# Eight tile buffers instead of five for the four-wide products, and another ring slot for the first prefetched unit

## What is computed

```python
x = layernorm(x + adj @ (scale[:, None] * (adj @ (x @ w0))) + bias)              # layer 0: two products with adj
x = layernorm(x + relu((inv_deg[:, None] * A1) @ x @ W.T + b))                     # layer 1: one
d = rsqrt(rowsum(adj)); z = leaky_relu((d[:, None] * (adj @ (d[:, None] * x))) @ W1 + b1)
S = exp(-sqrt(pairwise_squared_distances(z)) / 2), only the 4 nearest of each row kept
A2 = S + adj; d2 = rsqrt(rowsum(A2))
x = layernorm(x + (d2[:, None] * (A2 @ (d2[:, None] * x))) @ W2 + b2)             # layer 2: two, and a search
x = layernorm(x + relu(concat(x, adj @ x) @ W.T + b))                             # layer 3: one
```

## Time and profile before

| | us |
|---|---|
| median of three runs (lowest, highest) | 1589.72 (1587.08, 2805.07) |
| the profiled execution | 1597.85 |
| its span, first to last instruction | 1596.3 |
| TensorE busy (share of the span) | 1446.2 (91%) |
| VectorE busy | 836.0 (52%) |
| mean granted TensorE clock | 0.972 of full speed |

### The profile page before, as it was taken

The page is one execution under the profiler, slowest core; times in us unless marked ns, Lnnn a source line. Parts: engine busy times, 40 slices in busy tenths (PEclk is TensorE's granted clock), DMA queues, the critical chain, the costliest instruction groups (busy, mean ns, idle before and its releaser), DMA issues.

```text
span 1596.3 us, 20924 instructions
## 1 busy us (share of the span) xinstructions
PE 1446.2 (91%) x7300; PEld 748.6 (47%) x7300; DVE 836.0 (52%) x1278; ACT 465.3 (29%) x979; POOL 208.9 (13%) x267
## 2 busy tenths in 40 slices
PE   6888888887999999999999888999999499878997
PEld 4555555554444444444444433444444144433554
DVE  6667667664222133323222379999998046543122
ACT  4656565653000000000000056666665000000010
POOL 1111111110000000000000000000000447763000
PEclk9999999999999999999999999999999799989999
DMA  9999998888899888888777500013333889889773
GB/s 312 332 334 340 340 323 314 311 323 332 340 343 345 335 314 312 316 324 331 304 283 283 184 7 1 14 54 120 123 124 115 283 321 371 310 321 361 284 284 130
DMA packets 127677, 418.98 MB, mean 262 GB/s; under 512 B 10657, under 2 KB 44033, under 8 KB 104577
## 3 DMA queue, kind: packets, MB, share of 16 engines
q1 hardware_dynamic: 78272, 331.37, 55.9%
q0 software_dynamic: 19088, 71.83, 11.8%
q10 hardware_dynamic: 30256, 15.00, 3.2%
HBM read 353.14 MB, written 65.01 MB: 262 GB/s over the span
## 4 chain that ended last, share of the span: by engine, by line
PE 56%; DVE 16%; DMA 10%; issue 7%; POOL 5%; ACT 5%; DVEq 0%; ACTq 0%; POOLq 0%; SPq 0%
PE acc L1010 12%; PE acc L1011 12%; PE acc L1012 12%; POOL gath_all L434 5%; DVE hT L865 5%; DVE wz_sb L866 5%; DMA at_scratch<-region 4%; PE pt L1054 3%; DMA gath_all<-y_scratch,wz_sb 2%; DVE region L818 2%; PE pt L1116 2%; PE pt L1119 2%; PE pt L1118 2%; PE pt L1117 2%; PE pt L1012 2%
## 5 line engine op out<-in xcount | busy, mean ns | idle before, releaser
L1010 PE MATMUL acc<-region,yop 128*128 128x512 f16 x850 | 326.8, 385 | 63.7 <-DVE region L818 39.1
L1011 PE MATMUL acc<-region,yop 128*128 128x512 f16 x850 | 326.2, 384 | 0.0
L1012 PE MATMUL acc<-region,yop 128*128 128x512 f16 x850 | 325.8, 383 | 0.0
L592 ACT ACTIVATE region<-pt 128x512 f32<-128x512 f32 x256 | 149.8, 597 | 114.8 <-PE pt L1119 79.6
L818 DVE SCALAR_TENSOR_TENSOR region<-pt,region 128x512 f16<-128x512 f32 x200 | 128.9, 685 | 94.2 <-ACT region L499 93.5
L1054 PE MATMUL pt<-ident,region 128*128 128x128 f32 x1024 | 153.7, 278 | 8.3 <-DMA region<-in_adj 8.3
L1010 PEld LDWEIGHTS acc<-region,yop 128*128 128x128 f16 x850 | 83.6, 98 | 156.1 <-DVE region L818 51.2
L1054 PEld LDWEIGHTS pt<-ident,region 128*128 128x128 f32 x1024 | 129.7, 144 | 55.2 <-issue 9.5
L865 DVE MAX8 hT<-region 128x8 f32<-128x4096 f32 x32 | 141.5, 4421 | 11.4 <-ACT region L592 10.6
L499 ACT ACTIVATE region<-pt 128x512 f16<-128x512 f32 x200 | 112.6, 593 | 106.9 <-PE pt L1054 64.1
L1012 PEld LDWEIGHTS acc<-region,yop 128*128 128x128 f16 x850 | 83.9, 99 | 102.9 <-issue 4.4
(11 more groups left out here) (221 smaller groups left out, 1904.7 us busy)
## 6 DMA issues: line engine op xcount, KB each, us to landing
region<-at_scratch SPq DMA_DIRECT2D x180, 1280.0 KB, 7.3
region<-in_adj SPq DMA_DIRECT2D x64, 1024.0 KB, 9.0
at_scratch<-region POOLq DMA_DIRECT2D x40, 768.0 KB, 7.1
region<-at_scratch SPq DMA_DIRECT2D x100, 256.0 KB, 3.7
at_scratch<-region POOLq DMA_DIRECT2D x40, 512.0 KB, 7.5
x_scratch<-xout ACTq DMA_DIRECT2D x24, 256.0 KB, 6.2
yop<-in_x SPq DMA_DIRECT2D x4, 512.0 KB, 10.8
xin<-in_x POOLq DMA_DIRECT2D x8, 256.0 KB, 3.5
```

The source lines that it names most:

```text
L592: nc.scalar.activation(near[i % 2][:, j * CHUNK:(j + 1) * CHUNK], pt[n % NEAR_BANKS][:, :], ACT.Copy).then_inc(near_copied, 1)
L1010: nc.tensor.matmul(into, y[:, 0, kt, :], high, start=(kt == 0), stop=False)
L1011: nc.tensor.matmul(into, y[:, 0, kt, :], low, start=False, stop=False)
L1012: return nc.tensor.matmul(into, y[:, 1, kt, :], high, start=False, stop=(kt == KT - 1))
```

## The change

Three more tile buffers: the SBUF tensors `xin`, `xout` and `t_nat` (each 2 KB per partition, as large as a tile) are viewed as tiles 5 to 7. They are free from the end of pass 3 (the wait `zT_read >= NCH`) until the residual work after the four-wide products. The loads of the tiles keep their order, and tile n now waits for the use of tile n - 8 instead of n - 5.

The ring slots of the late units are renamed: the first unit of chunk 4 goes to slot 4, the third to slot 2 (they were 2 and 4); the others of pass 4 stay (slot 3, 0, 1). The first of them now waits for `near_used >= 31` instead of 32. In pass 5 the slots are exchanged in the same way, 2 for 4.

```diff
-TILE_SLOTS = 5
+REGION_TILES = 5
+TILE_SLOTS = 8
+LATE_ORDER = [4, 3, 2, 0, 1]
...
         tiles = [region[:, s * tile_elems:(s + 1) * tile_elems].rearrange("p (h n) -> p h n", h=2)
-                 for s in range(TILE_SLOTS)]
+                 for s in range(REGION_TILES)]
...
+        tiles = tiles + [held[:, :, :].rearrange("p t f -> p (t f)").bitcast(F16).rearrange("p (h n) -> p h n", h=2)
+                         for held in (xin, xout, t_nat)]
+        assert len(tiles) == TILE_SLOTS
...
         def late_slot(p, c, u):
             if p == 4:
-                return (u + 2) % UPC
-            return (c + 2) % UPC if c < WIDE else (u + 1) % UPC
+                return LATE_ORDER[u]
+            return LATE_ORDER[c] if c < WIDE else LATE_ORDER[(u + WIDE) % UPC]
...
                     n = (kt - KEPT) * WIDE + c
+                    if n == REGION_TILES:
+                        sp.wait_ge(zT_read, NCH)
                     if n >= TILE_SLOTS:
                         sp.wait_ge(tile_used, n - TILE_SLOTS + 1)
...
                 if kt in LATE_AT:
-                    sp.wait_ge(near_used, KT)
+                    sp.wait_ge(near_used, KT - 1 if LATE_AT[kt] == 0 else KT)
                     load_late(LATE_AT[kt])
```

More of the change, by code:

```diff
@@ L100, in gnn_kernel @@
         tiles = [region[:, s * tile_elems:(s + 1) * tile_elems].rearrange("p (h n) -> p h n", h=2)
-                 for s in range(TILE_SLOTS)]
+                 for s in range(REGION_TILES)]
         def chunk_buffer(s):
-            at = (TILE_SLOTS + s) * tile_elems
+            at = (REGION_TILES + s) * tile_elems
             return region[:, at:at + tile_elems].bitcast(F32).rearrange("p (t f) -> p t f", t=TPC)
@@ L108, in gnn_kernel @@
         yw = [chunk_buffer(2 + s) for s in range(2)]
-        assert (TILE_SLOTS + 4) * tile_elems <= near_end - 4 * N
+        assert (REGION_TILES + 4) * tile_elems <= near_end - 4 * N
         yop = [sb(f"yop{b}", [P, 2, KT, D], F16) for b in range(2)]
```

## The result

| | before | with the change |
|---|---|---|
| median of 20 runs, us | 1595.4 | 1583.44 |
| ratio, 95% interval | | 0.992 (0.990 to 0.994) |
| profiled execution, us | 1597.85 | 1583.6 |
| kt 24's first product to the end of kt 31, us | 48.9 | 32.6 |
| from there to the end of the kernel (**the rest** below), us | 314.0 | 317.0 |

The kernel is 0.8% faster: less than 2%, but clear of its noise. The gain of the profiled pair is 14.3 us, of which 1.0 is an earlier start of the stretch, 16.3 a shorter stretch, and -3.0 a longer rest; by the medians it is 12.0 us. One of the twenty runs of the kernel before took 2805.07 us; without it the median is 1594.55.

A forecast was written before the change was run, and what follows sets the result against it. From kt 24 to kt 31 TensorE waits for tiles queued behind large units, and all later work hangs on that end. Moving 10.3 MB at 335 GB/s saves 14.9 us: 1589.7 - 14.9 = 1574.8, say 1575, range 1567 to 1584.

The forecast's parts named there:

- rival A: Kt 24 to 31: only the first stop's cost returns, stops at two later units keep their length; 7.8 us less, chance 0.16.
- The first unit earlier, at no cost.: Under the search's last step: chunk 4's first unit issued at about 1224.5 instead of 1235.87, costing nothing, VectorE undisturbed.
- No stop before 1243, then 3 to 6 us ahead of kt 28, and one ahead of kt 30.: TensorE from kt 24: early stops of 1.35 and 5.01 us go; two remain, at the later units.
- The sum by transfers: From 1236 to kt 31's end: 10.3 MB left at 335 GB/s, ending at 1267.4 instead of 1282.3, 14.9 us less.
- above 300 throughout: Expected sign: DMA rate above 300 GB/s all the way from 1236 to the end of kt 31, at about 1267.
- B: From about 1248, TensorE stays at its 1.2 GHz clock and becomes the bound; 13.5 us less, 1576.2, chance 0.10.
- C: Transfer rates near 400, capped by GpSimd's idle time; 20 to 25 us less, 1565 to 1570, chance 0.08.
- D: No effect: the queue reaches the unit no earlier, or the gather chain returns the gain; 1588 to 1592, chance 0.07.
- E: Slower: chunk 0's gathers land late in a continuous jam, 18 us being the threshold; 1598 at 22 us, chance 0.04.
- The shift passes on whole.: Behind kt 31: GpSimd keeps some 10 us of its 25.43 us wait, so the earlier end reaches the kernel's end in full.
- the sign of a wrong sum: From kt 31's end to the kernel's end: 314 us changing by more than 3 us would show the sum wrong.
- The base: Whole kernel before the change: the median of 1589.72 us from which the gain was subtracted, with three runs varying some 3 us.

The follow-up runs named there:

- buffers only: Changed kernel with eight tile buffers, but chunk 4's units in their old slots and the first unit waiting for the search's last step again; ratio 0.9926 to the kernel before.
- slots only: Changed kernel with five tile buffers as before, keeping the changed ring slots and the first unit's earlier wait; ratio 0.9997 to the kernel before.
- all rows of 2 KB: Changed kernel with the scratch rows of residual sums and of x after layers 0, 1, 2 side by side, 2048-byte pieces; ratio 0.9862 to the kernel before.

## Why the prediction was right, and where it was not

The time lay in the range (1567 to 1584), but only just: 1583.44 is 0.6 us from its upper end, outside the forecast's own 1571 to 1578, and nearer to rival A's 1581.9 than to the 1575. That it fell inside owes as much to the width kept for A as to the forecast. The mechanism is the forecast's all the same, as the trace shows step by step:

- *The first unit earlier, at no cost.* Right: issued at 1223.86 (forecast 1224.5), and VectorE's two last search steps kept their 4.42 us. What it buys was mis-sized. The sum took 1.31 MB out of the stretch, 3.9 us at 335 GB/s; buffers only showed 2.0 to 2.6. The reason for costing the slot by itself was right too: it stands behind tile 75, and without the buffers it is worth nothing (0.9997), since the queue, not the search, held the unit.
- *No stop before 1243, then 3 to 6 us ahead of kt 28, and one ahead of kt 30.* A stop of 1.37 us was left in kt 26; then 4.11 and 1.33 us. Right but for the first.
- *The sum by transfers:* 335 GB/s, the end at 1267.4, 34.0 us from kt 24 on. Measured 336 GB/s, 1265.0, 32.6 us, with 397 GB/s in its fullest stretch. The Trainium skill, DMA: Bandwidth & Descriptors, "Where 436 GB/s comes from", gives about 358 GB/s as the limit of the HBM side; no such limit shows here, as the row of 403 had said. The rate is right and the end to 2.4 us; "above 300 throughout" failed for the last 5 us (221). That the rivals fell is in the same rows: the stops at the later units shortened from 6.29 and 7.06 us to 4.11 and 1.33 (A), the granted clock was back at full by 1260 (B), the stretch moved by 16.3 us (C wanted over 20, D none), and the gathers of chunk 0 landed in 5.6 us at most, where E needed 18. But the rule behind the sum is narrower than I wrote. With one unit behind kt 30 and the other behind the last tile, 1.31 MB less stood ahead of the last tiles, and nothing was gained; with both behind the last tile it was 7.9 us.
- *"The shift passes on whole."* This is the step that failed. GpSimd's idle time (8.54 us, forecast 10) and `mix(0)` (10.1 us behind the end, forecast 10.0) are right, and the rest was then taken as a constant of 314 us. It is not one: 314.0 and 318.1 with five buffers, 317.0 and 320.9 with the change. The first pair differs by 3.0 us, just the 3 that I had named as the sign of a wrong sum, and the second trace is beyond it. In the rest VectorE waits, in most traces once for long, for a residual sum that shares the DMA engines with units twenty times its piece size. The runs with other piece sizes shorten that wait or take it away, and bring the rest to 302.5 to 309.4 us. How much of the 2.9 us between 14.9 forecast and 12.0 measured is this wait, and how much the profiled execution's distance from the median, the few traces don't settle. With the units behind the last tile it is plain in the trace: of 7.9 us gained, 7.8 were given back.
- *The base.* The three runs shown had a median of 1589.72; twenty have 1595.4. Of the 8.4 us between forecast and measured time, 5.7 are this. One of the three was the 2805.07, so the base stood on two ordinary runs, and a spread of 3 us for them was too small.

## What to carry to other kernels

Where a large transfer is queued between small ones that an engine consumes one by one, count buffers in time: they must cover the large transfer, and a wait taken off an instruction helps only if nothing in front of it on its queue is held. When a gain in one stage vanishes in the next, look for a wait whose place moves from run to run; here it was a small transfer on another queue, and it cost most where little of the chain was left to make it up. Compare the piece sizes of the queues that share the engines before giving such a transfer more lead.

## What the runs showed of the hardware that was not expected

- A load of 256 KB in pieces of 512 bytes took up to 30.6 us (3.0 at best) beside a queue with pieces of 10240, and up to 31.3 with slots only; at 2048 against 10240 the longest was 17.0 to 17.4, at 512 against 2048 it was 17.0. I had looked for such a thing only in the gathers, which land in 5.5 to 6.1 us (median, 1265 to 1460 us) in all traces that show their landings.
- Splitting a unit into five DMAs of 256 KB cost the DMA engines some time, but the kernel none that shows: from 1290 to 1420 us they moved 359 GB/s at a busy share of 1.03 in that run, against 369 at 0.95 with all rows of 2 KB and whole units. The 332 of the changed kernel (0.90) hold its pauses.
- A stop of 4 us still cost the clock, a shorter one did not. With the change the granted clock was 0.50, the lower of its two levels, from 1250 to 1254, behind the 4.11 us, and 1.00 from 1260 on, behind the 1.33. Over the stretch it was 0.88, before the change 0.78 (1236 to 1282), and with the units behind the last tile, with no stop above 0.7 us, 1.00.
